# An eighth turned expert in position 1, and a first state tile prepared one step further at each place

## The chip, the cores and the metric

The kernel runs on one core of one Trainium2 chip. The metric is the time of one execution on the device, in microseconds; the median of three runs is 1242.97 us (1241.31 to 1243.07). The trace that is read here comes from one profiled execution of 1242.44 us.

## The reference, cut to what matters

The input is `x` of shape (4, 1024, 128) in float32. Three parts follow each other, each with a layer norm in front and a residual sum behind:

```python
x = x + 0.5 * ffn(layernorm(x))      # mixture of 8 experts
x = x + mamba(layernorm(x))          # a state-space layer with 16 states
x = x + 0.5 * ffn(layernorm(x))      # the same mixture again

# ffn
router = softmax(x @ w_router); gate = softmax(x @ w_gating / 0.1)
g = x @ w_gate[e]; u = x @ w_up[e]              # 128 -> 512, for each of 8 experts
expert_out[e] = (silu(g) * u) @ w_down[e]       # 512 -> 128
cw = router * gate / (sum(router * gate) + 1e-9)
out = sum over e of expert_out[e] * cw[e]

# mamba
xs, z = split(x @ W_in)                         # 256 channels each
xc = silu(causal_conv4(xs) + conv_b)
dt, B, C = split(xc @ W_x); dt = softplus(dt @ W_dt + b_dt)
h[t] = exp(dt * A) * h[t-1] + dt * xc * B       # 256 channels x 16 states, over 1024 steps
y = (sum over states of h * C + xc * D) * silu(z);  out = y @ W_out
```

## The kernel before, in words

**Tiles and positions.** The 4096 rows of `x` are eight tiles of 512 rows. Each tile goes through the mixture twice, which makes 16 positions; `ORDER` says which mixture (0 or 1) of which tile stands at each, and it starts with tiles 0 and 1 of the first mixture. A position has 8 experts of 4 slots each, so 32 slots; a slot is one chunk of 128 of the 512 inner columns. Experts are counted through: expert 8 is the first of position 1, with slots 32 to 35.

**A slot.** TensorE makes the gate product (`first_g`, L996 to L999) two slots ahead and the up product (`first`) of its own slot, each as three products of rounded float32 parts (high by high, low by high, high by low); ScalarE applies silu (`silu`, L1555); VectorE multiplies by the up product (`h`, L1345). The down product of a slot comes two slots later (`down`), in one of two forms. Not turned, it is 4 float32 products, 8 records of 128 columns in the trace at L1105. Turned, its result is transposed, and it is three products of 512 columns on rounded parts (L1097, L1099, L1101); for these the activations are split into a high part (`h_hi`, ScalarE L1566 or VectorE L1295) and a low part (`h_lo`, VectorE L1301), and each pair of slots splits its down weights (`wd_hi` L1572 or L1308, `wd_lo` L1313).

**Turned experts.** `TURNS` names them per position: before, experts 1 to 5 of position 0, 1 to 7 of position 1, all 8 of position 14 and 0 to 6 of position 15. The weighing of a turned expert (`acc`, L1279) multiplies by rows of router weights: after the position's weights are known they are transposed (`cw_t`, L1124), stored to DRAM (`cw_store`, L960) and loaded again, spread over all partitions, once per turned expert (`cw_load`, L967) into the ring `YE` of two buffers. The first turned expert of a position writes its product into `AT` itself; the others are added to `AT` by a transfer that GpSimd issues (L1721). At the end `AT` is transposed back and added to the rows (`t_tr` L1134, `t_add` L1290). An expert that isn't turned is weighed by L1338 or L1580 and added to `XT` by a transfer of the same size.

**The state-space layer.** For tile t the stream `before(t)` prepares it: layer norm, four products with `W_in` (`b_in`), the convolution (`b_conv`, L1396), silu, the product with `W_x` (L1148), the store and loads of B and C (L948, L955), the product with `W_dt` (L1155, L1156), softplus and `b_dx` (L1408). Then `scans(t)` takes over: for each state n a product (`s_b`, L1426), two scans (L1437), a product (`s_hc`, L1445), and the exponentials `s_da` on ScalarE (L1643, a table load and 4 instructions for two states).

**What sets the order.** The function `timetable()` writes one list of steps, and each engine's program is that list filtered to its own steps; every engine runs its part in order, with semaphores between. `timetable()` keeps an estimated clock for each engine, and the side streams (prep, before, scans, closing, rows, turn) are generators. `side()` is called after each gate, each up and each down of a slot. It advances the mixture's side streams; the stream `before` is otherwise advanced by `fill()`, and only while VectorE's estimated clock is less than about 1.4 us ahead of TensorE's. Steps that need a bank for small products share a single one (`NB` is 1), which `take()` hands out.

`WEIGHED_LATER` puts the weighing of a turned expert behind the next expert's second down, and of the first of a position (`BEGIN_LATER`) behind the third. SP's program holds the row loads and the loads of B and C in the order of the list, with waits for the store and for a free buffer.

Of the kernel before, what the change touches and what calls it, by code (L numbers as in the profile page):

```python
# [51 lines left out]
LATEST = 0.2  # L52
SIGNAL = {"pe": .14, "v": .12, "a": .15, "p": .1}
BURST = 2
HURRY = 0
QUICK = [("x2", NT - 1)]
FIRST_BY_VECTOR = (2, 3, 1)
SPARE = 1.0
# [14 lines left out]
NORMED = 5.0  # L73
PATIENCE = 25.0

TURNS = {0: range(1, 6), 1: range(1, 8), 14: range(0, 8), 15: range(0, 7)}
EASY = 0.8
SPLIT = 2
SPLITS = TURNS
TURNED = [p * E + e for p in TURNS for e in TURNS[p]]  # L80
SPLIT_EXPERTS = [p * E + e for p in SPLITS for e in SPLITS[p]]
TURN_BEGINS = {p * E + TURNS[p][0]: p for p in TURNS}
TURN_ENDS = {p * E + TURNS[p][-1]: p for p in TURNS}
SUMMING = (NPOS - 2, NPOS - 1)
TURN_SUMS = {p * E + TURNS[p][-1]: p for p in TURNS if p in SUMMING}
TURNED_SLOTS = {g * FC + c: k * FC + c for k, g in enumerate(SPLIT_EXPERTS) for c in range(FC)}
# [14 lines left out]
def timetable():  # L101
# [9 lines left out]
    def step(*what, after=0.0, **work):  # L111

        steps.append(what)
        for e, c in work.items():
            clock[e] = max(clock[e], after) + c
            after = clock[e] + SIGNAL[e]
        return after
# [62 lines left out]
    def prep(p):  # L180
# [29 lines left out]
        at = step("p_cw", p, after=at, v=.35)  # L210
        if p in TURNS:
            streams["rows"] = weights_rows(p, at)
# [32 lines left out]
    def weights_rows(p, at):  # L245
        yield from until(at + ROWS)
        bk = yield from take()
        at = step("cw_t", p, bk, after=at, pe=.15, a=.3)
        give(bk[0], "a_ct", list(TURNS).index(p) + 1, at)
        step("cw_store", p)  # L250
        rows_at[p] = at + 1.0
# [196 lines left out]
    def advance(k):  # L448
        if k not in streams:
            return None  # L450
        w = next(streams[k], "end")
        if w == "end":
            del streams[k]
        return w
# [17 lines left out]
    def side(but=None):  # L472
# [6 lines left out]
        turn[0] += 1  # L479
        if HURRY and "scans" not in streams and not begun["scans"]:  # L480
            advance("before")
# [1279 lines left out]
```

## Time and profile before

| what | value |
|---|---|
| median of 3 runs | 1242.97 us |
| the profiled execution | 1242.44 us |
| its span | 1240.6 us |
| TensorE busy | 1233.1 us (99%) |
| VectorE busy | 1143.4 us (92%) |
| ScalarE busy | 1003.6 us (81%) |
| GpSimd busy | 446.4 us (36%) |
| granted TensorE clock | 1.00 throughout |
| scans of tile 0 start | 161.49 us |

Times in the trace count from the start of the span. An engine's busy time is the union of its instructions; a matmul's end is modelled, so a short wait between two products can hide under a busy record and is better read from the starts of neighbouring products. The execution lies 0.5 us under the median of the three runs.

### The profile page before, as it was taken

Reading aid. Unit: us, or ns where it says so; the run is one execution under the profiler, and the core shown is the slowest. Engines: PE = TensorE matmul, PEld = TensorE weight load, DVE = VectorE, ACT = ScalarE, POOL = GpSimd, SP = SyncE. Lnnn points to the kernel's source line nnn. Section 1 sums busy time; section 2 is a strip of 40 time slices with the busy share of each in tenths; the row PEclk is TensorE's granted clock in tenths of the full one; section 3 lists DMA queues with packets and bytes.
Section 4 is the critical chain, followed back from the end, with each engine's and each line's share of the span. In section 5 each row is a group of like instructions: output and inputs, shape, how many; then the busy total and the mean of one; then the engine's idle time right before and its main releaser. Section 6 shows DMA issues by size and latency. Waiting matters only on the chain.

```text
span 1240.6 us, 20186 instructions
## 1 busy us (share of the span) xinstructions
PE 1233.1 (99%) x7072; PEld 1058.2 (85%) x7072; DVE 1143.4 (92%) x1368; ACT 1003.6 (81%) x2122; POOL 446.4 (36%) x571
## 2 busy tenths in 40 slices
PE   9999999999999999999999999999999999999999
PEld 7787788888888888888888888888888888887887
DVE  6958899999999999999999999997999999978877
ACT  7678789798898898988879898797988978846654
POOL 1021134445453463453434434452444344402000
PEclk9999999999999999999999999999999999999999
DMA  8412458888788997987889887986688979932322
GB/s 227 111 27 45 105 116 174 165 171 167 162 176 178 183 187 157 198 170 165 181 180 187 166 196 160 191 181 138 131 166 169 196 169 194 182 63 43 74 48 60
DMA packets 121015, 184.84 MB, mean 149 GB/s; under 512 B 11344, under 2 KB 38096, under 8 KB 120912
## 3 DMA queue, kind: packets, MB, share of 16 engines
q0 software_dynamic: 53568, 97.54, 45.0%
q1 hardware_dynamic: 67344, 86.00, 26.6%
q8 instruction: 56, 0.92, 0.3%
q14 instruction: 47, 0.39, 0.1%
HBM read 83.30 MB, written 2.69 MB: 69 GB/s over the span
## 4 chain that ended last, share of the span: by engine, by line
PE 93%; DVE 3%; ACT 2%; issue 1%; DMA 1%; SPq 0%; DVEq 0%; ACTq 0%
PE PS L1105 28%; PE PS L996 19%; PE PS L999 18%; PE PS L997 18%; PE PS L1101 2%; PE PS L1097 2%; PE PS L1099 2%; PE PS L1163 1%; PE PS L1148 1%; DVE HB L1345 1%; PE PS L1032 1%; DVE HL L1301 1%; PE PS L1040 1%; DMA YE<-CWD 1%; PE PS L1003 0%
## 5 line engine op out<-in xcount | busy, mean ns | idle before, releaser
L1105 PEld LDWEIGHTS PS<-WD,HB 128*128 128x128 f32 x3200 | 393.9, 191 | 22.1 <-issue 2.0
L1105 PE MATMUL PS<-WD,HB 128*128 128x128 f32 x3200 | 395.9, 275 | 0.0
L1345 DVE TENSOR_TENSOR HB<-PS,HB 128x1024 f32<-128x1024 f32 (+1 forms) x336 | 322.9, 962 | 72.5 <-PE PS L999 56.7
L1555 ACT ACTIVATE HB<-PS 128x512 f32<-128x512 f32 x512 | 294.9, 596 | 95.5 <-PE PS L999 93.5
L1733 POOL DMA_DIRECT2D Y<-HS x252 | 221.8, 954 | 317.6 <-DMA Y<-HS 151.7
L996 PE MATMUL PS<-XH,WG 128*128 128x512 f32 x509 | 219.7, 432 | 0.3 <-ACT HB L1555 0.2
L996 PE MATMUL PS<-XH,WU 128*128 128x512 f32 x512 | 204.4, 399 | 0.4 <-DVE HB L1345 0.4
L999 PE MATMUL PS<-XH,WU 128*128 128x512 f32 x512 | 201.2, 393 | 0.0
L999 PE MATMUL PS<-XH,WG 128*128 128x512 f32 x509 | 200.7, 394 | 0.1
L997 PE MATMUL PS<-XH,WU 128*128 128x512 f32 x512 | 200.4, 391 | 0.0
L997 PE MATMUL PS<-XH,WG 128*128 128x512 f32 x509 | 199.3, 392 | 0.0
L1721 POOL DMA_DIRECT2D XT<-YE x99 | 96.6, 976 | 197.7 <-ACT YE L1580 84.9
L1643 ACT ACTIVATE DA<-XS,aneg 128x512 f32<-128x512 f32 x256 | 164.1, 712 | 1.6 <-DVE HS L1437 1.0
L1437 DVE TENSOR_TENSOR_SCAN HS<-DA,car,HS 128x512 f32<-128x512 f32 x128 | 160.3, 1272 | 0.0
L1445 DVE TENSOR_TENSOR HS<-BCB,HS 128x1024 f32<-128x1024 f32 x128 | 156.3, 1221 | 2.4
L1426 DVE TENSOR_TENSOR HS<-BCB,DX 128x1026 f32<-128x1026 f32 (+1 forms) x128 | 155.8, 1221 | 1.6 <-DMA BCB<-BCD 1.5
L1437 DVE TENSOR_TENSOR_SCAN HS<-DA,HS 128x513 f32<-128x513 f32 x128 | 152.8, 1219 | 0.9 <-ACT DA L1643 0.8
L1566 ACT ACTIVATE HI<-HB 128x512 fp32r<-128x512 f32 x102 | 64.4, 632 | 76.1 <-DVE HB L1345 73.0
L996 PEld LDWEIGHTS PS<-XH,WU 128*128 128x128 f32 x512 | 96.1, 188 | 25.2 <-DVE HB L1345 3.1
L997 PEld LDWEIGHTS PS<-XH,WU 128*128 128x128 f32 x512 | 96.3, 188 | 21.7 <-issue 0.7
L999 PEld LDWEIGHTS PS<-XH,WU 128*128 128x128 f32 x512 | 96.1, 188 | 21.8
L999 PEld LDWEIGHTS PS<-XH,WG 128*128 128x128 f32 x509 | 95.5, 188 | 22.2 <-DVE XH L1403 0.5
(164 smaller groups left out, 1572.9 us busy)
## 6 DMA issues: line engine op xcount, KB each, us to landing
BCB<-BCD SPq DMA_DIRECT2D x128, 512.0 KB, 5.2
Y<-HS POOLq DMA_DIRECT2D x252, 256.0 KB, 6.0
XT<-YE POOLq DMA_DIRECT2D x99, 256.0 KB, 5.1
YE<-CWD SPq DMA_DIRECT2D x27, 256.0 KB, 4.5
AT<-YE POOLq DMA_DIRECT2D x21, 256.0 KB, 3.3
WD<-in_L_ffn_w_down_dram SPq DMA_DIRECT2D x8, 256.0 KB, 6.0
XT<-in_L_attn_x_dram SPq DMA_DIRECT2D x7, 256.0 KB, 5.8
out_dram<-XT SPq DMA_DIRECT2D x7, 256.0 KB, 5.4
```

Of the source, the lines that this page charges most:

```text
L996: pe.matmul(o, w[0], m[0], start=True, stop=False)
L997: pe.matmul(o, w[1], m[0], start=False, stop=False)
L999: pe.matmul(o, w[0], m[1], start=False, stop=True).then_inc(S[sem], 1)
L1105: z = pe.matmul(part(g, j), HB[:, i % NH, j * P:(j + 1) * P], WD[:, e, c, :], start=c == 0 and j == 0, stop=c == FC - 1 and j == SUB - 1)
L1345: v.tensor_tensor(H, PS[:, NG + i % 2:NG + i % 2 + n, :], H, ALU.mult).then_inc(S["v_h"], 1)
L1426: v.tensor_tensor(HS[:, m % HR, :, 0:w], rows.unsqueeze(1).broadcast_to([P, 2, w]), DX[:, t % 2, :, 0:w], ALU.mult).then_inc(S["v_db"], 1)
L1437: v.tensor_tensor_scan(H, DA[:, m % NA, j, 0:w], H, car[:, j, n:n + 1] if t % 2 else 0.0, ALU.mult, ALU.add).then_inc(S["v_sc"], 1)
L1445: v.tensor_tensor(H, BCB[:, m % BR, 1, :].unsqueeze(1).broadcast_to([P, 2, T]), H, ALU.mult).then_inc(S["v_hc"], 1)
L1555: a.activation(HB[:, i % NH, :], gate(i), ACT.Silu).then_inc(S["a_sil"], 1)
L1643: z = a.activation(DA[:, m % NA, j, 0:T], XS[:, t % 2, j, 3:3 + T], ACT.Exp, scale=aneg[:, j, n:n + 1])
L1721: gp.dma_start(to, buffer(g), accum_op=ALU.add).then_inc(S["c_acc"], 16)
L1733: gp.dma_start(Y[:, t % 2, j, :], HS[:, m % HR, j, 0:T], accum_op=ALU.add).then_inc(S[f"c_y{j}"], 16)
```

## The change

Two constants change. `TURNS[1]` becomes `range(0, 8)`, so expert 8 (slots 32 to 35) is turned as well: its down products take the other form, its activations and down weights are split, the first row load of position 1 is for expert 8, expert 8 writes `AT` at first, and expert 9 is added by a transfer to `AT`. Everything that is derived from `TURNS` follows. `HURRY` becomes 1, which makes a branch of `side()` live: as long as no scans stream exists and none has begun, each call of `side()` advances `before` by one step. The stream `before(1)` doesn't exist until scans have begun, so this is the preparation of state tile 0 alone.

```diff
-HURRY = 0
+HURRY = 1
...
-TURNS = {0: range(1, 6), 1: range(1, 8), 14: range(0, 8), 15: range(0, 7)}
+TURNS = {0: range(1, 6), 1: range(0, 8), 14: range(0, 8), 15: range(0, 7)}
```

The branch that it makes live stands in `side()`:

```python
        if HURRY and "scans" not in streams and not begun["scans"]:
            advance("before")
        elif "scans" in streams and (haste or turn[0] % (EVERY if passed[0] < SOONER else 1) == 0):
            advance("before")
        fill(clock["pe"] + LEAD + 1.0)
```

## Rows read from the trace of the kernel before

**Rows 1.** The page: span, busy time of the engines, the chain's shares, two groups.

```profile
span 1240.6 us, 20186 instructions
PE 1233.1 (99%) x7072; PEld 1058.2 (85%) x7072; DVE 1143.4 (92%) x1368; ACT 1003.6 (81%) x2122; POOL 446.4 (36%) x571
...
PE 93%; DVE 3%; ACT 2%; issue 1%; DMA 1%; SPq 0%; DVEq 0%; ACTq 0%
...
YE<-CWD SPq DMA_DIRECT2D x27, 256.0 KB, 4.5
```

**Rows 2.** Windows of the whole core: length, then busy us by engine, clock, DMA.

```profile
80.00:160.00 80.00, 78.96 (x368) 63.17 (x366) 65.02 (x124) 64.51 (x141) 13.72 (x27) 1.00 0.28 63
160.00:1080.00 920.00, 918.98 (x5594) 804.65 (x5594) 891.63 (x893) 795.90 (x1691) 403.19 (x493) 1.00 0.85 173
1080.00:1240.00 160.00, 157.08 (x752) 129.35 (x750) 128.14 (x228) 87.66 (x174) 20.03 (x29) 1.00 0.31 61
```

**Rows 3.** The chain in order of time: start, length, what; down products of two slots.

```profile
163.61 1.79 PE PS L1105 x16
```

**Rows 4.** Timeline where position 1 ends: start, length, instruction, [idle before <- releaser].

```profile
157.34 1.22 DVE L1426 TENSOR_TENSOR HS<-BCB,DX 128x1026 f32<-128x1026 f32 x1
157.85 0.39 PE L1097 MATMUL PS<-HI,WDS 128*128 128x512 f32 x1
158.47 1.22 DVE L1345 TENSOR_TENSOR HB<-PS,HB 128x1024 f32<-128x1024 f32 x1
158.53 0.39 PE L1097 MATMUL PS<-HI,WDS 128*128 128x512 f32 x1
158.75 2.56 ACT L1643 ACTIVATE DA<-XS,aneg 128x512 f32<-128x512 f32 x4
158.75 0.39 PE L1099 MATMUL PS<-HI,WDS 128*128 128x512 f32 x1
159.61 0.68 DVE L1301 TENSOR_TENSOR HL<-HB,HI 128x512 fp32r<-128x512 f32 x1
160.34 0.50 PE L1101 MATMUL PS<-HL,WDS 128*128 128x512 f32 x1 [1.20 <-DVE HL L1301]
```

**Rows 5.** Groups of VectorE by form, 90 to 155 us: busy, mean ns, idle before.

```profile
L1345 DVE TENSOR_TENSOR HB<-PS,HB 128x512 f32<-128x512 f32 x27 | 18.6, 687 | 11.8 <-PE PS L999 11.8
L1301 DVE TENSOR_TENSOR HL<-HB,HI 128x512 fp32r<-128x512 f32 x26 | 17.7, 682 | 0.0
L1313 DVE TENSOR_TENSOR WDS<-WD,WDS 128x256 fp32r<-128x256 f32 x14 | 6.0, 429 | 0.3
```

**Rows 6.** Position 0: its first row load and who waits for it, timeline of 30 to 44 us.

```profile
38.53 0.69 DVE L1279 TENSOR_TENSOR AT<-PS,YE 128x512 f32<-128x512 f32 x1 [1.11 <-DMA YE<-CWD]
39.75 0.39 PE L1099 MATMUL PS<-HI,WDS 128*128 128x512 f32 x1
40.48 0.50 PE L1101 MATMUL PS<-HL,WDS 128*128 128x512 f32 x1 [0.34 <-DVE HL L1301]
```

**Rows 7.** Position 1: store and first load of rows, VectorE from 100 us on, first use.

```profile
95.07 0.32 SPq L960 DMA_DIRECT2D CWD<-LR  x1
96.53 0.36 SPq L967 DMA_DIRECT2D YE<-CWD  x1
...
100.33 0.68 DVE L1301 TENSOR_TENSOR HL<-HB,HI 128x512 fp32r<-128x512 f32 x1
111.49 0.68 DVE L1279 TENSOR_TENSOR AT<-PS,YE 128x512 f32<-128x512 f32 x1
```

**Rows 8.** The preparation of state tile 0, and ScalarE's first burst of exponentials.

```profile
109.62 0.74 DVE L1396 SCALAR_TENSOR_TENSOR Y<-XS,cw_t,Y 128x512 f32<-128x512 f32 x1
113.95 0.74 DVE L1396 SCALAR_TENSOR_TENSOR Y<-XS,cw_t,Y 128x512 f32<-128x512 f32 x1
150.20 1.22 DVE L1408 TENSOR_TENSOR DX<-XS,Y 128x1024 f32<-128x1024 f32 x1
157.45 1.28 ACT L1643 ACT_TABLE_LOAD   x1
```

## The prediction

> **What bounds the kernel now.** I read the page first: TensorE is busy 1233.1 of 1240.6 us and has 93% of the chain that ended last, so 7.5 us of the span at most are waits that show as idle time [rows 1]. The windows say where they lie: 1.04 us in 80 to 160 us, only 1.02 us in the 920 us after it, 2.9 us in the last 160 [rows 2]. VectorE is the second full engine, at 97% from 160 to 1080 us, but only 81% in 80 to 160 us [rows 2]: this is position 1's stretch, where the change sits, and nearly all of VectorE's idle time there ends when a TensorE product is done (11.8 us, before `h`) [rows 5]. So VectorE waits for TensorE here, and the time follows TensorE: its work, plus every wait that gets through to it. Waits are read from neighbouring starts: where a third down product follows its second by more than 0.23 us, the rest is lost.
>
> **Part 1, expert 8 turned: what goes.** Two slots of the unturned down take 1.79 us [rows 3], so 0.895 us a slot. A turned slot takes from 157.85 to 158.53, 0.68 us for its three products [rows 4]. Four slots: 4 x 0.215 = 0.86 us less on TensorE, which is the path. Nothing is late in their place by itself, since the gate and up products of the next slots are already at hand in order.
>
> **Part 1, what comes on VectorE and ScalarE.** Four low parts of the activations, 4 x 0.68, and two low parts of down weights, 2 x 0.43, are 3.6 us on VectorE [rows 5]; the high parts go to whichever engine the timetable finds free. They fall between 80 and 93 us. VectorE has 15 us idle in 80 to 160 us [rows 2], a share of 19%, so some 2.5 us in those 13 us and 3.6 wanted: it becomes full there, for 1 us of lag at most, and a `h` or a low part has about 1 us of room before the third product wants it. I cost it at 0.1 us; bounds are 0 and, if that cover is gone, one wait like the largest in position 1, 159.61 to 160.34 behind a late low part, 1.36 us by starts (1.59 - 0.23) [rows 4]. Transfers are a wash: expert 8's transfer to XT goes and expert 9's to AT comes, one issue each on GpSimd; SP gets one row load more.
>
> **Part 1, a wait that is added.** This is the term that I looked at longest. Before, the first row load of position 1 was issued at 96.53, landed about 4.5 us later, and was used only at 111.49 [rows 7, 1]: ten microseconds of room. Now it serves expert 8, weighed behind the third down of expert 9, that is behind the low part that ran at 100.33 and ended about 100.93 [rows 7]. With TensorE 0.86 us ahead, VectorE arrives at 100.1. The store is triggered by a step with a due time 4 us behind the router weights, so it moves little: the load lands at 101.0. VectorE waits 0.9 us. Queued behind it in order are the weighing, state tile 0's low part (`b_xl`), a weight split and the `h` and low part of the next slot, for which TensorE's down waits. Position 0 has the same figure: VectorE waited 1.11 us for its first row load, and TensorE then lost 40.48 - 39.75 - 0.23 = 0.50 us [rows 6]. Bounds: 0 (the store moves forward by the same 0.86 us, and no wait is left) and 1.0 (a second wait of that size in the wake). I take 0.35 us, scaled from position 0 by 0.9/1.11 and rounded down for the earlier store.
>
> The store of the rows is followed by its load after 96.53 - 95.07 = 1.46 us, since SP waits for the landing [rows 7]. The Trainium skill, in "DMA: Bandwidth & Descriptors", section "Anatomy of one DMA — SWDGE (gpsimd) path", gives any DMA a fixed cost of about 2.0 us, heaviest where the target is HBM, as here. By that rule the pair would land 0.5 us later, the wait of VectorE would be 1.4 us and the term 0.6 instead of 0.35; this trace's store is quicker than the page has it, and it is the same store, so the row decides.
>
> **Part 2, `HURRY`.** It removes and adds no instruction. It moves the steps of `before(0)` ahead of others in the queues of VectorE, ScalarE and TensorE, and on SP the store and first loads of B and C ahead of a row load or two. How far: the first two taps of the convolution, which need nothing of each other, stand 4.3 us apart (109.62, 113.95) [rows 8], because `fill()` stops when VectorE's clock is ahead. With a step at each call they come some 0.7 us apart, and the third product with `W_in` gets the bank before the next position's preparation does. From 113.95 to the end of the preparation at 150.20 [rows 8] are 36 us for work of which VectorE's share is small. I estimate the preparation done 8 to 12 us earlier. But scans can run then only in VectorE's idle time, and that is 15 us in the window less 3.6 for part 1, so all of the state-space work gains at most 11 us, and I count with 5. What is that worth? From 160 to 1080 us TensorE loses 1.0 us in all [rows 2]: an earlier state-space layer has nothing to give to an engine that doesn't wait for it. It can only give back waits near the place itself. The largest of them is at the end of position 1: VectorE began `s_b` of the second state at 157.34, the doubled `h` behind it started at 158.47 and the low part at 159.61, and TensorE's third product came 1.36 us late [rows 4]. Without that `s_b` in front, `h` could start about 1.0 us earlier. If the hurried order puts it elsewhere 1.0 us is gained; but a doubled `h` with a low part behind it stands at this border anyway, and some scan work will stand near it. On the other side the scans of tile 0 now start inside turned slots, of which rival C tells. Bounds: -1.4 (that wait gone) and +4.1 (rival C). I take 0, between them and nearest to the windows, where the larger part of the scans' 920 us costs TensorE nothing.
>
> The one other cover that I lean on is the shared SP queue: row loads wait for a free buffer and loads of B and C stand behind them. Before, the first use of a row load came 10 us after its landing [rows 7], so a load or two of B and C ahead of one is hidden; gone, it would be a wait like position 0's, 0.50 us [rows 6].
>
> **Part 3, everything behind.** The timetable is greedy, so all later choices (which engine weighs, where a burst of exponentials stands) may fall otherwise. The work stays. The waits there are 1.0 + 2.9 us [rows 2]; I expect their sum back within 0.6 us either way.
>
> **The sum**, against the profiled execution, 1242.44 us, span 1240.6: -0.86 + 0.1 + 0.35 + 0 = -0.41, so 1242.0 and a span of 1240.2. That execution is 0.53 us below the median of the three runs; on the median it is 1242.97 - 0.41 = 1242.6. I predict 1242.5.
>
> **Rivals.**
> A. The row load is in time, and the border's wait goes: -0.86 + 0.1 - 1.2 = -2.0, 1241.0. For it: VectorE has 15 us idle in the window. Against: position 0's first load was late in the same construction [rows 6]. Chance 0.21.
> B. The row load costs its upper bound and the splits theirs: -0.86 + 1.0 + 1.36 = +1.5, 1244.5. For it: a full queue on VectorE with `b_xl` just behind. Against: VectorE was idle half a microsecond or more before most `h` in this stretch [rows 5]. Chance 0.13.
> C. Slower. The scans of tile 0 begin inside position 1, and with them ScalarE's bursts of exponentials: a table load of 1.28, 2.56 for four and, to return to silu, a second load of the same kind, 5.1 us in which no silu and no high part is made [rows 8, 4]. A turned slot needs ScalarE for both, and TensorE's products for two slots are shorter by 2 x 0.215 us. The single burst so far that touches turned slots is the one at 157.45, and the largest wait in position 1 stands beside it [rows 4]. Decays for two states at a time are allowed up to three states ahead of the scans, so up to three bursts can come before slot 64: 3 x 1.36 = 4.1. With the sum's other terms 1242.97 - 0.41 + 4.1 = 1246.7. It decides from about 2.9 us of added waits on, two bursts at full price and a bit. Against: the timetable hands high parts to VectorE when ScalarE is behind, and the wait at 160.34 is named after VectorE. Chance 0.13.
> D. `HURRY` doesn't do what it says: `before` was advanced at nearly every place already, or the one bank holds it, and scans start where they did. Then the sum is part 1's alone, 1242.6 as well. Chance 0.10. My forecast has the other 0.43.
>
> **How the numbers follow.** A measurement of this kernel can tell about 0.2% from no change, 2.5 us: below 1240.5 is faster, above 1245.5 slower. The forecast, D and B lie between. Of A's 0.21 I put 0.10 below 1240.5, where also waits behind 160 us get fewer. Of C 0.12 lies above 1245.5, of B 0.02. Faster 0.10, same 0.76, slower 0.14. The range goes from 1240.4 (the removed work, the border's wait and 0.4 of part 3) to 1245.6 (B's bounds and part of C), which leaves 0.1 out at either end.
>
> **What would show it.** Right: 16 L1105 records fewer per two slots, 32 in all, and 4 more each of L1097, L1099, L1101, L1301; L1279 of expert 8 at 100 to 101 us with idle time that ends on YE<-CWD; a gap of about 0.5 us between a second and third down product before 105 us; DX (L1408) at 138 to 143 instead of 150.20; all of the state-space work up to 5 us earlier and the window 160 to 1080 us as full as before. Wrong: gaps of over 1 us at third down products between 135 and 160 beside L1643 (C); the gap at the border gone with the first load in time (A); DX where it was (D); or TensorE's idle time behind 160 us grown by more than 0.6 us, which no part of this sum has.

## The result, and the profile after

| | before | after |
|---|---|---|
| median, 4 runs each | 1242.55 us | 1258.26 us |
| lowest and highest | 1241.31, 1243.07 | 1252.23, 1258.55 |
| profiled span | 1240.6 us | 1256.5 us |
| mean granted clock of TensorE | 1.00 | 0.996 |

The ratio is 1.0116, with a 95% interval of 1.0085 to 1.0148. By the medians it is slower by 15.7 us, where 1242.5 was forecast and 1245.6 was the upper end of the range. One of the four runs took 1252.23 us, at a clock of 0.997.

The page of the kernel after, its lines that answer to [rows 1] (busy time of each engine; the chain of waits by engine):

```profile
span 1256.5 us, 20163 instructions
...
PE 1237.4 (98%) x7052; PEld 1059.0 (84%) x7052; DVE 1150.4 (92%) x1383; ACT 1001.6 (80%) x2116; POOL 453.3 (36%) x571
...
PE 69%; DMA 11%; DVE 7%; ACT 6%; issue 4%; POOL 2%; SPq 0%; DVEq 0%; POOLq 0%; ACTq 0%
```

TensorE's busy time grew by 4.3 us although 0.86 us of work is gone, and the rest of the 15.9 us is idle time. The chain that ended last now runs through transfers for 11% of the span, 1% before. The windows answer to [rows 2], cut finer (length; busy us of PE, PEld, VectorE, ScalarE, GpSimd; clock; DMA share; GB/s):

```profile
80.00:120.00 40.00, 36.40 (x161) 28.81 (x160) 27.71 (x57) 26.98 (x65) 4.76 (x11) 0.96 0.13 32
120.00:160.00 40.00, 39.84 (x170) 30.82 (x170) 35.33 (x70) 31.53 (x71) 7.63 (x15) 1.00 0.31 64
160.00:200.00 40.00, 33.57 (x181) 28.68 (x180) 30.87 (x33) 28.82 (x59) 11.77 (x13) 0.91 0.55 116
200.00:1096.00 896.00, 892.81 (x5432) 780.52 (x5432) 872.14 (x874) 772.14 (x1636) 402.96 (x487) 1.00 0.85 174
```

Two windows of 40 us hold most of it, and only these two have a clock under 1.00. VectorE's waits from 80 to 200 us, longest in total first, name what is late (who waits, for whom: us in total, times, longest):

```profile
DVE HB L1345 <- PE PS L999: 12.2, 15, 1.6
DVE YE L1279 <- DMA YE<-CWD: 5.4, 1, 5.4
DVE AT L1279 <- DMA YE<-CWD: 4.1, 1, 4.1
DVE aneg L1370 <- ACT aneg L1584: 1.4, 1, 1.4
```

The first line is VectorE waiting for TensorE, in 15 short waits. Both long waits are loads of router rows: the first of position 1 (expert 8's), which the forecast had at 0.9 us, and one for expert 14, which it had at nothing.

**The first wait.** SP's, VectorE's and TensorE's timelines of the kernel after, around expert 8's weighing:

```profile
97.83 0.32 SPq L960 DMA_DIRECT2D CWD<-LR  x1
...
104.15 0.40 PE L999 MATMUL PS<-XH,WU 128*128 128x512 f32 x1
105.89 0.69 DVE L1279 TENSOR_TENSOR AT<-PS,YE 128x512 f32<-128x512 f32 x1 [4.10 <-DMA YE<-CWD]
106.63 0.50 PE L1097 MATMUL PS<-HI,WDS 128*128 128x512 f32 x1 [2.08 <-DVE AT L1279]
106.97 0.40 PE L1099 MATMUL PS<-HI,WDS 128*128 128x512 f32 x1
107.83 0.64 PE L1101 MATMUL PS<-HL,WDS 128*128 128x512 f32 x1 [0.46 <-DVE HL L1301]
108.27 0.63 PE L996 MATMUL PS<-XH,WG 128*128 128x512 f32 x1
108.70 0.63 PE L997 MATMUL PS<-XH,WG 128*128 128x512 f32 x1
```

and the chain of waits there (start, length, what):

```profile
97.83 3.49 DMA CWD<-LR
101.32 0.01 issue
101.33 4.53 DMA YE<-CWD
```

The store started 2.8 us later than before and took 3.49 us against 1.46 [rows 7]; the load behind it took its usual 4.5. By starts TensorE loses 106.63 - 104.15 - 0.23 = 2.25 us, since the down product wants the bank that the weighing empties, and 107.83 - 106.97 - 0.23 = 0.63 behind the next low part. Then eight products start 0.43 us apart instead of 0.23 (108.27, 108.70): the granted clock has gone from its level of 2.4 GHz to that of 1.2 GHz, for 1.6 us more. A third wait stands ahead of them: VectorE waited 1.37 us at 90.42 behind a table load on ScalarE, and TensorE lost 1.2 us at 90.72.

**The second wait.** SP's, VectorE's and TensorE's timelines of the kernel after, where position 1 ends:

```profile
151.03 0.32 SPq L948 DMA_DIRECT2D BCD<-XN  x1
152.66 1.39 SPq L955 DMA_DIRECT2D BCB<-BCD  x3
154.09 13.68 SPq L967 DMA_DIRECT2D YE<-CWD  x2
...
164.37 0.39 PE L1099 MATMUL PS<-HI,WDS 128*128 128x512 f32 x1
167.57 0.69 DVE L1279 TENSOR_TENSOR YE<-PS,YE 128x512 f32<-128x512 f32 x1 [5.36 <-DMA YE<-CWD]
168.18 1.22 DVE L1408 TENSOR_TENSOR DX<-XS,Y 128x1024 f32<-128x1024 f32 x1
169.31 1.22 DVE L1345 TENSOR_TENSOR HB<-PS,HB 128x1024 f32<-128x1024 f32 x1
170.45 0.68 DVE L1301 TENSOR_TENSOR HL<-HB,HI 128x512 fp32r<-128x512 f32 x1
171.19 0.79 PE L1101 MATMUL PS<-HL,WDS 128*128 128x512 f32 x1 [6.43 <-DVE HL L1301]
171.78 0.63 PE L996 MATMUL PS<-XH,WG 128*128 128x512 f32 x1
172.21 0.63 PE L997 MATMUL PS<-XH,WG 128*128 128x512 f32 x1
```

The row load of 256 KB was issued right behind three loads of B and C of 512 KB each, and landed 13.46 us later, at 167.55. VectorE waited 5.36 us with `b_dx`, a doubled `h` and a low part queued behind, so TensorE lost 171.19 - 164.37 - 0.23 = 6.59 us, and then some 2.1 at the lower clock. The product that waited is the last one of slot 63, behind the doubled `h` and its low part: the place where the kernel before lost 1.36 us [rows 4]. So 5.2 us of the 6.59 are new.

Why not before? The same stretch of the kernel before, SP and VectorE:

```profile
139.03 0.32 SPq L948 DMA_DIRECT2D BCD<-XN  x1
140.88 1.38 SPq L955 DMA_DIRECT2D BCB<-BCD  x3
142.31 1.33 SPq L967 DMA_DIRECT2D YE<-CWD  x1
...
156.74 0.68 DVE L1279 TENSOR_TENSOR YE<-PS,YE 128x512 f32<-128x512 f32 x1
```

The load was slow there too: it landed at 151.96, 9.65 us after its issue, and was used at 156.74, so it had 4.8 us of room. In the kernel after VectorE was ready for this weighing at 162.21 (167.57 - 5.36), 5.5 us later than before. But the load was issued 11.8 us later (154.09 for 142.31) and took 3.8 us longer, so it came 10.1 us later against the weighing; 4.8 of these were room, the rest is the wait.

It was issued late because SP runs its list in order. The buffer of this load was free at 146.60, when the transfer of expert 12 landed that GpSimd had issued at 143.31. But the store of B and C stands ahead of the load, and that one went out at 151.03 instead of 139.03. So the load was held for 7.5 us, where it was held for 1.8 in the kernel before (the transfer issued at 137.26 landed at 140.54).

**The account.** TensorE's lost time, from the starts of neighbouring products minus the median spacing of their kind, in us by window:

| kernel | 0–80 | 80–120 | 120–160 | 160–200 | behind 200 | sum |
|---|---|---|---|---|---|---|
| before | 1.9 | 0.2 | 1.9 | 0.5 | 2.7 | 7.2 |
| after | 2.2 | 6.2 | 0.7 | 9.0 | 5.6 | 23.7 |

The difference is 16.4 us; with 0.86 us of removed work that leaves 15.6, and the spans differ by 15.9. The windows are of time and not of work: slot 63's wait lies in 120 to 160 us before and in 160 to 200 us after.

### The profile page after: what moved, and what is told of

Read it like the earlier page. It is cut to its first block, busy times and chain, and to the rows that moved or that the text cites. A ratio compares the mean times of both kernels' runs of the same rounds, so it can differ in the third digit from the quotient of the medians.

```text
span 1256.5 us, 20163 instructions
## 1 busy us (share of the span) xinstructions
PE 1237.4 (98%) x7052; PEld 1059.0 (84%) x7052; DVE 1150.4 (92%) x1383; ACT 1001.6 (80%) x2116; POOL 453.3 (36%) x571
## 4 chain that ended last, share of the span: by engine, by line
PE 69%; DMA 11%; DVE 7%; ACT 6%; issue 4%; POOL 2%; SPq 0%; DVEq 0%; POOLq 0%; ACTq 0%
PE PS L1105 19%; PE PS L996 14%; PE PS L999 14%; PE PS L997 14%; DMA Y<-HS 7%; DVE HB L1345 2%; DMA YE<-CWD 2%; PE PS L1101 2%; PE PS L1097 1%; PE PS L1099 1%; DMA XT<-YE 1%; DVE HS L1437 1%; ACT DA L1643 1%; ACT HB L1555 1%; PE PS L1148 1%
## 5 line engine op out<-in xcount | busy, mean ns | idle before, releaser
L1105 PEld LDWEIGHTS PS<-WD,HB 128*128 128x128 f32 x3168 | 389.3, 191 | 20.9 <-issue 1.5
L1105 PE MATMUL PS<-WD,HB 128*128 128x128 f32 x3168 | 391.0, 275 | 0.0
```

Source lines behind the costliest of these rows:

```text
L1105: z = pe.matmul(part(g, j), HB[:, i % NH, j * P:(j + 1) * P], WD[:, e, c, :], start=c == 0 and j == 0, stop=c == FC - 1 and j == SUB - 1)
```

## The experiments

The explanation to test: the time went into two waits of VectorE for row loads, each of which also costs clock; the one in 80 to 120 us comes from expert 8 and its late store, the one behind 160 from the three loads of B and C ahead of the row load. Rivals: the bursts of exponentials inside turned slots (rival C of the prediction), VectorE too full by expert 8's splits, and the replanned order as such. The ratios stand against runs of the kernel before on the same chip.

| kernel | median us | ratio, 95% | 80–120 | 120–160 | 160–200 | behind 200 |
|---|---|---|---|---|---|---|
| expert 8 alone | 1253.46 | 1.0091 [1.0076, 1.0106] | 6.2 | −0.2 | 5.0 | 5.7 |
| `HURRY` alone | 1258.54 | 1.0129 [1.0114, 1.0144] | 0.4 | 8.3 | 6.5 | 5.6 |
| after, two B/C loads later | 1252.23 | 1.0092 [1.0066, 1.0118] | 4.1 | 0.6 | 2.7 | 6.5 |
| after, expert 8's rows ahead | 1252.53 | 1.0082 [1.0067, 1.0097] | 1.5 | 6.6 | 1.8 | 5.5 |
| both of these | 1247.96 | 1.0039 [1.0025, 1.0053] | 1.4 | 1.7 | 4.1 | 3.1 |
| `HURRY` alone, B/C loads later | 1252.1 | 1.0073 [1.0058, 1.0088] | 0.4 | 2.1 | 5.4 | 5.2 |
| before, replanned only | 1245.58 | 1.0019 [1.0010, 1.0028] | 0.2 | 1.8 | 0.4 | 3.4 |
| expert 8, order kept | 1243.07 | 0.9999 [0.9991, 1.0008] | 0.7 | 2.0 | 0.4 | 3.4 |
| the same, border moved | 1241.81 | 0.9990 [0.9981, 0.9999] | 0.6 | 1.0 | 0.4 | 3.3 |
| border moved alone | 1241.94 | 0.9994 [0.9985, 1.0002] | 0.2 | 0.8 | 0.5 | 2.7 |

The last four columns are the lost time of the profiled execution in us, as above. Four runs of one kernel lie up to 7.7 us apart here ("after, two B/C loads later": 1250.26 to 1257.92), and the medians of different chips stand side by side, so single microseconds between two rows say little.

**Each half alone.** The kernel after with `-HURRY = 1` / `+HURRY = 0`:

> Expert 8 turned, HURRY back to 0. Theory 1 (late row loads): the loss comes from row loads that land after VectorE has reached the weighing that needs them, once at expert 8 (4.10 us of wait in the kernel after) and once at expert 14, whose load stands in SP's queue behind the first three loads of B and C (5.36 us). Without HURRY the preparation of tile 0 ends later still, so the three loads of B and C come a few us later and stand before the load of expert 15 instead: a wait of the same kind there. 1250 to 1260 us. Rival (the hurried order does the damage, by filling VectorE's and ScalarE's queues in turned slots): the sum of my prediction without it, 1242 to 1244 us. DX (L1408) at 165 us or later in both.

and the kernel after with position 1's experts as before:

```diff
-TURNS = {0: range(1, 6), 1: range(0, 8), 14: range(0, 8), 15: range(0, 7)}
+TURNS = {0: range(1, 6), 1: range(1, 8), 14: range(0, 8), 15: range(0, 7)}
```

> HURRY 1, expert 8 not turned. Theory 1: no row load is used early here; the first one of position 1 serves expert 9, ten microseconds after landing, and the loads of B and C are issued about 10 us earlier, when the row load behind them has some 8 us of room. 1241.5 to 1244 us, no wait over 0.5 us of VectorE on YE<-CWD, DX (L1408) at 138 to 143 us. Rival (the hurried order): most of the loss is here, 1250 us or more, at third down products between 135 and 160 us.

Neither half is harmless: 1.0091 and 1.0129. For `HURRY` alone 1241.5 to 1244 us had been expected, and that was missed. Expert 8 alone has both waits, the second at expert 15. VectorE's timeline of that kernel:

```profile
105.49 0.69 DVE L1279 TENSOR_TENSOR AT<-PS,YE 128x512 f32<-128x512 f32 x1 [4.26 <-DMA YE<-CWD]
169.25 0.69 DVE L1279 TENSOR_TENSOR YE<-PS,YE 128x512 f32<-128x512 f32 x1 [5.66 <-DMA YE<-CWD]
169.85 1.22 DVE L1408 TENSOR_TENSOR DX<-XS,Y 128x1024 f32<-128x1024 f32 x1
```

So `b_dx`, the end of tile 0's preparation, goes from 150.20 [rows 8] to 169.85 by expert 8 alone, and `HURRY` takes back 1.7 us of it (168.18). But in both kernels `b_dx` stands on VectorE behind the second wait, and some 5.5 us of the delay are that wait itself. The store of B and C, issued ahead of that wait, tells how late the preparation is: 139.03 before, 154.41 with expert 8 alone, 151.03 after. SP's, VectorE's and TensorE's timelines of `HURRY` alone:

```profile
129.69 0.32 SPq L948 DMA_DIRECT2D BCD<-XN  x1
131.32 1.39 SPq L955 DMA_DIRECT2D BCB<-BCD  x3
132.75 1.36 SPq L967 DMA_DIRECT2D YE<-CWD  x1
144.37 0.69 DVE L1279 TENSOR_TENSOR YE<-PS,YE 128x512 f32<-128x512 f32 x1 [4.25 <-DMA YE<-CWD]
145.64 1.22 DVE L1408 TENSOR_TENSOR DX<-XS,Y 128x1024 f32<-128x1024 f32 x1
167.63 1.23 DVE L1437 TENSOR_TENSOR_SCAN HS<-DA,HS 128x513 f32<-128x513 f32 x1 [2.77 <-ACT DA L1643]
170.62 0.80 PE L1101 MATMUL PS<-HL,WDS 128*128 128x512 f32 x1 [3.41 <-DVE HL L1301]
```

Alone it does what it says, and about as far as the prediction had it: the store of B and C goes out 9.3 us earlier (129.69 for 139.03). `b_dx` itself gains only 4.6 (145.64 for 150.20), since the wait of 4.25 us stands in front of it. And being early breaks the fit too: the B and C loads move to 131.32, ahead of a row load that is wanted at 140, and it lands at 144.34. Its buffer was free at 124.16, so it was held for 8.6 us. Behind it a scan beside turned slots waits 2.77 us for its exponentials, with a doubled `h` and its low part queued behind. That is rival C's mechanism, once, for 3.57 us of TensorE at 166.83, again at slot 63, where 1.36 had been lost before.

**The B and C loads.** The kernel after with one load of B and C ahead of the row load instead of three:

```diff
-            bc_loads(BR)
+            bc_loads(1)
```

> The kernel after, but of the first three loads of B and C only one is issued ahead of the row loads of experts 14 and 15, the other two behind them. Nothing else in any engine's order changes. Theory 1: the wait at expert 14 (5.36 us of VectorE, 6.59 us by starts on TensorE, and the half clock behind it, some 2.2 us) goes: 1258.3 - 8.8 = 1249.5; perhaps 1 us of it returns, because the second product of the scans now waits for its load. 1248.5 to 1252 us. Rival (ScalarE's burst of exponentials beside that wait is the cause): unchanged, 1257 to 1259.

SP's and TensorE's timelines of this kernel:

```profile
104.11 0.40 PE L999 MATMUL PS<-XH,WU 128*128 128x512 f32 x1
106.11 0.50 PE L1097 MATMUL PS<-HI,WDS 128*128 128x512 f32 x1 [1.61 <-DVE AT L1279]
...
150.54 0.36 SPq L955 DMA_DIRECT2D BCB<-BCD  x1
150.94 6.79 SPq L967 DMA_DIRECT2D YE<-CWD  x2
157.78 3.14 SPq L955 DMA_DIRECT2D BCB<-BCD  x2
```

The second wait is gone (of VectorE's waits for row loads from 80 to 200 us only the first is left, 3.6 us), with 6.3 us of lost time in 160 to 200 us, and slot 63 loses 1.12 us, where the kernel before loses 1.36. The median falls by 6.0 us; the slowest of the four runs still took 1257.92. The row load landed 5.21 us after its issue, at 156.15, and was used at 160.01. This edit moves only those two loads, so without them ahead of the row load there is no wait. It doesn't follow that they alone make it: the row load was held behind the late store here too, for 6.4 us. Issued at 146.60 in the kernel after, even a landing time of 13.46 us would have brought it at 160.1, before the 162.21 at which VectorE wanted it (an estimate from the two kernels' rows). So by this estimate both were needed, the late store and the loads behind it. A row load ahead of the store was not tried. The first wait, 1.77 us by starts here, cost no clock in this execution, the quickest of the kernel's four. The same edit on the kernel with `HURRY` alone:

> HURRY alone, with two of the first three loads of B and C behind the next row loads. HURRY alone took 1258.5: a wait of 4.25 us of VectorE at L1279 for a row load issued at 132.75 behind those three (5.6 us by starts on TensorE), 3.6 us at the end of position 1 where a scan waits for exponentials, the half clock after both, and 3 us behind 300 us. Theory 1: the first goes, with its half clock some 7 us: 1251.5; the other stays. 1249 to 1253 us. Rival (the hurried steps fill VectorE's queue, the row load only happened to be late there): 1256 to 1259.

It takes 6.2 us from 120 to 160 us and 6.4 us from the time, and here all four runs (1250.82 to 1252.8) lie below all four without the edit (1258.1 to 1259.85). The wait of the scan for its exponentials stays, with 3.57 us of TensorE, now at 161.27.

**The first row load.** In the kernel after, expert 8 is weighed with position 0's rows, which are long in DRAM, loaded ahead of the store:

```diff
                 elif s[0] == "cw_store":
+                    if s[1] == 1:
+                        wt.wait_ge(S["c_ct"], 16)
+                        wait_buffer(wt, E)
+                        rows = CWD[0].rearrange("(j e) p -> e j p", e=E)[1:2]
+                        sy.dma_start(buffer(E), rows.broadcast_to([P, SUB, P])).then_inc(S[rows_loads(E)[0]], 16)
...
+                elif s[0] == "cw_load" and s[1] == E:
+                    pass
```

> The kernel after, but expert 8's rows are loaded from the rows that position 0 stored, so ahead of position 1's store and not behind its landing; expert 8 is weighed with position 0's weights, a part of the output that this kernel leaves wrong. No other instruction moves. Theory 1: the wait of 4.10 us at L1279 goes, and with it 2.25 + 0.63 us by starts on TensorE and the half clock behind (8 products at 0.2 us more, 1.6 us): 1258.3 - 4.5 = 1253.8. The later wait at expert 14 stays. Rival (VectorE is simply full between 100 and 107 us): 1257 to 1259.

80 to 120 us falls from 6.2 to 1.5 us of lost time: the first wait was the row load's, and the clock fell behind it. The second wait stays, and only changes its window: its row load, again behind three loads of B and C, goes from 149.30 to 162.28, and TensorE loses 6.12 us from 159.56 on, where after lost 6.59 from 164.37 on. The median falls by 5.7 us (runs 1251.25 to 1255.41). With both edits:

> The kernel after with both edits at once: expert 8's rows taken from position 0's store, ahead of position 1's (expert 8 is weighed with position 0's weights, which this kernel leaves wrong), and two of the first three loads of B and C behind the row loads of experts 14 and 15. Theory 1 (late row loads plus the half clock behind them are the loss): alone they gave 6.0 and 5.7 us back; what is left over the kernel before is 1.2 us at 90 us, where VectorE waits for ScalarE's table loads, 1.1 us at the end of position 1, and some 4 us of new waits behind 400 us, less 0.86: 1247.5 to 1250 us, granted clock 1.00. Rival (the waits are replaced by others, since VectorE and ScalarE are full there): 1252 or more, as each edit alone.

1247.96 us, 10.3 us less than after, with every run below every run of after: 4.5 us are left over the runs of before on the same chip, of 15.7. The two waits with their clock are some two thirds of the loss. What is left is a wait of 1.2 us at 89.79, one of 2.47 at 167.58 (the closing transposition waits for a transfer to `AT`), and small ones; the 1.14 at 158.80 are slot 63's, which the kernel before has too. The wait of 2.47 may come from the edit: the transfer of expert 14 was issued at 157.55, beside the two loads of B and C that were moved, and took 8.8 us instead of 3.3, and the last transfer was issued only behind it, at 166.91.

**The replanned order.** The kernel before with one constant that only shifts where the planner calls `before` once scans run:

```diff
-EVERY = 3
+EVERY = 4
```

> The kernel before with one constant of the timetable moved, EVERY 3 to 4: no expert more is turned and no step is hurried; the order is the same up to 190 us and falls otherwise behind. It measures what a replanned order costs by itself. Theory 2 (the kernel before has an order that was picked for having hardly a wait, and nearly any other has more): 1244 to 1248 us, with 2 to 5 us of new waits before L1032, L1345 or L996 spread over positions 3 to 13. Rival (the order is robust, the late waits of the kernel after come from its late state-space layer): 1242 to 1243.5.

The ratio is 1.0019 [1.0010, 1.0028] over 10 runs, some 2.4 us, for a new order alone; its profiled execution shows 0.9 of them as lost time. The kernel after has waits of that kind, at places that the change doesn't touch. At 445.33, for one, TensorE waits 1.06 us for a normed tile (L1032, behind ScalarE's L1525).

The kernel after and five of the experiments on it or on one half lose 5.2 to 6.5 us behind 200 us, where before loses 2.7; the one with both waits off (3.1) and the control (3.4) lose less. The kernel with both waits off has the same order behind 200 us as the kernel after, since its edits move only row loads and loads of B and C ahead of that. So the 2.9 us that after loses there more than before aren't a fixed price of its order; how much of them is the order's, and how much follows from what came before, is open. The control shows that a new order alone can cost time, 1.2 to 3.5 us by its interval.

**Expert 8 with the order kept.** The planner's list of the kernel before, into which expert 8's steps are put by hand (behind the named step, the new ones):

```diff
+    behind = {("down", 29): [("wd_hi", 32), ("wd_lo", 32)],
+              ("h", 32, 1): [("h_hi", 32)],
+              ("h", 33, 1): [("h_hi", 33), ("h_lo", 32, 1)],
+              ("h", 34, 1): [("h_lo", 33, 1), ("h_hi", 34)],
+              ("down", 32): [("wd_hi", 34), ("wd_lo", 34)],
+              ("h", 35, 1): [("h_lo", 34, 1), ("h_hi", 35)],
+              ("h", 36, 1): [("h_lo", 35, 1)],
+              ("h_lo", 40, 1): [("acc", 8)]}
```

> Expert 8 turned inside the order of the kernel before: its steps are inserted by hand into the old timetable (row load first behind the store, weighing behind the low part of slot 40), and no other step moves. Theory: the 0.86 us of TensorE work come back in full, since the row load lands at 101 us and VectorE reaches the weighing at 102 to 103, and the 3.6 us of VectorE work fit its idle time; no replanned order, so no new wait behind. 1241.5 to 1242.0 against 1242.6. Rival (turning expert 8 costs waits wherever it is put, as position 1 has no room on VectorE): 1243 to 1246.

The ratio is 0.9999 [0.9991, 1.0008], over 11 runs; the 0.6 to 1.1 us less that were expected don't show. But the work of expert 8's turn isn't what costs, and neither is a full VectorE. SP's and VectorE's timelines of this kernel:

```profile
98.19 0.91 SPq L967 DMA_DIRECT2D YE<-CWD  x2
...
104.20 0.68 DVE L1279 TENSOR_TENSOR AT<-PS,YE 128x512 f32<-128x512 f32 x1
```

The load starts 3.1 us earlier than in the kernel after and the weighing finds it there. The 0.86 us of saved work are lost again in small waits (0.5 us more in 80 to 120, 0.7 behind 200, 0.4 ahead of 80).

**The border.** The forecast's largest wait of position 1 [rows 4], at slot 63, with `s_b` of the second state moved behind the last low part; on the kernel above, and alone:

```diff
+    steps.remove(("s_b", 0, 1))
+    steps.insert(steps.index(("h_lo", 63, 1)) + 1, ("s_b", 0, 1))
```

> Expert 8 turned inside the order of the kernel before, as in the run of that name, and one step more moved by hand: the product of the scans (L1426) that stood in front of the doubled `h` at the end of position 1 goes behind that `h` and the low part after it. The wait there (1.33 us by starts) shrinks by the 1.1 us that the product takes, and 0.86 us of TensorE work is gone: 1.0 us less than the run without the move and 1.0 to 1.9 us less than the kernel before (the run without the move showed the 0.86 us hardly or not: 0.9999 [0.9991, 1.0008]). Rival (what is gained at the border is lost a few slots on, because the first scan begins later): the same as the kernel before.

> The kernel before with that one step moved, nothing else. 1.0 us less than the kernel before, gap at the border about 0.3 us instead of 1.36, if that wait is worth what the gap says; the first scan starts at its old time, as it waits for the weighing of expert 15 and ScalarE's exponentials. Rival: no change.

TensorE's and VectorE's timelines of the border moved alone:

```profile
158.61 1.22 DVE L1345 TENSOR_TENSOR HB<-PS,HB 128x1024 f32<-128x1024 f32 x1
159.95 0.39 PE L1099 MATMUL PS<-HI,WDS 128*128 128x512 f32 x1
160.35 1.22 DVE L1426 TENSOR_TENSOR HS<-BCB,DX 128x1026 f32<-128x1026 f32 x1
160.49 0.50 PE L1101 MATMUL PS<-HL,WDS 128*128 128x512 f32 x1
```

The third product follows 0.54 us behind the second instead of 1.59: 1.05 us are gone there, and the time is 1.0 us below the 21 runs of before on that chip (1242.98), at an interval that still reaches 1.0002. With expert 8 it is 1.2 us, 0.9990 [0.9981, 0.9999]. That is the best version found, and 0.1% under the kernel before.

## Why the prediction was wrong

Three statements failed, two in Part 2 and one in Part 1.

1. *"I estimate the preparation done 8 to 12 us earlier."* It came later: the store of B and C by 12.0 us (151.03 for 139.03), of which some 5.5 are the lateness of the whole kernel by then, and `b_dx` by 18.0 (168.18, foreseen at 138 to 143), of which 5.4 are the second wait. For `HURRY` by itself the estimate was good (9.3 us at the store). What was missed is expert 8, which the prediction priced on the engines and not in the planner's clocks: with it alone the store is 15.4 us later. Already the first layer norm of the preparation (L1511) came at 99.75 instead of 89.24, and `b_xl` (L1376) at 121.31 instead of 100.93. How the delay passes through the planner is read from its code; no kernel tried it. `timetable()` holds back steps that need ScalarE while ScalarE's estimated clock is over 1 us ahead of TensorE's, and a high part enters that clock only once VectorE's clock has reached its `h`. So VectorE's clock, filled by the low parts, carries over. The lists fit this: `timetable()` puts `b_dx` at 150.7 on VectorE's clock in the kernel before and at 156.8 in the kernel after, at 149.0 if expert 8's low parts are given no time, and still at 156.8 if its high parts are given none.

2. *"Before, the first use of a row load came 10 us after its landing [rows 7], so a load or two of B and C ahead of one is hidden; gone, it would be a wait like position 0's, 0.50 us [rows 6]."* That room was read at the first load of position 1 and used for one that stands behind three B and C loads, which had 4.8 us. And the price was that of a load behind nothing. With 1.5 MB ahead of it the load took 9.65 us before and 13.46 after, and it was held behind the late store for 7.5 us instead of 1.8. TensorE lost 6.59 us, 5.2 more than before at this slot, plus 2.1 of clock, against a price of 0.50. Moving two of the three loads gave 6.0 us of the median back.

3. *"The store is triggered by a step with a due time 4 us behind the router weights, so it moves little: the load lands at 101.0."* It landed at 105.86. This is the first wait, and the term of +0.35 below.

By the other steps:

- **Removed work, −0.86:** right in its count (L1105 has 3168 records, 32 fewer). In time it is hardly there: expert 8 with the order kept lies 0.35 us below the runs of before on its chip (1243.42), and with the border moved expert 8 adds 0.13 us of gain, both inside the intervals.
- **Splits, +0.1:** the mechanism (VectorE lags) shows in none of the long waits, and the kernel with the order kept has only 0.5 us more lost in the window. Right to within that.
- **The first row load, +0.35 (bound 1.0):** the mechanism was right in place, instruction and releaser, and the size was wrong by more than ten: 2.25 + 0.63 us of waits and 1.6 of clock. The load did land 4.5 us after its issue. The step that failed is "it moves little": the store was issued 2.8 us later (97.83 for 95.07) and took 2.0 us more. The order kept gives the price without that: no wait at all. The Trainium skill's page "DMA: Bandwidth & Descriptors", section "Anatomy of one DMA — SWDGE (gpsimd) path", with its fixed cost of about 2.0 us, would have moved this term by 0.25 us only. The section describes transfers that GpSimd issues, and this store is one of SP's, which the prediction passed over. The store of the kernel after, at 3.49 us, lies above both that figure and the 1.46 us of before.
- **A term that was missing, the clock:** half speed behind both long waits, some 3.7 us together. The kernel before is at 1.00 throughout, so its rows could not price it.
- **Everything behind, ±0.6:** +2.9 us. The bound came from a kernel whose order had been left as it was; the replanned control costs 2.2 us by the medians, though its trace shows only 0.7 of it as lost time behind 200 us.
- **The border's wait:** rival A was right that it can go, for 1.05 us, when it is moved by hand. In the kernel after it didn't go: the second wait fell on the same product, the third of slot 63, and took it in. Rival C's mechanism exists, once, in `HURRY` alone. Rival D is refuted in the form in which it stood: `HURRY` does move the preparation.
- **TensorE's idle time behind 160 us grown by more than 0.6 us:** named as a sign of a wrong sum, and it came.

The accounting by parts: the first wait and its neighbours +6.0 us, 120 to 200 us with the second wait +7.3 (+8.5 and −1.2, as slot 63 changed its window), behind 200 us +2.9, before 80 us +0.3, work −0.86.

Open: why one run of the kernel after took 1252.23 us; the four runs of the kernel with two B and C loads later also lie between 1250.26 and 1257.92, at mean clocks of 1.000 and 0.996. So the clock may have fallen in some runs and not in others, but only one run of each kernel has a trace. Open as well is why the row load took 13.46 us after its issue and 9.65 before, behind the same three loads.

## What to carry to other kernels

In a statically planned kernel an edit of one stage is priced by what the planner's clocks do with it, not only by its instructions: put the edit into the old order by hand and compare, and run a replanned control. The room of a load is to be read at that load, with what stands ahead of it on its queue: both what holds back its issue and what slows its landing. A long wait on TensorE cost a further 1.6 to 2.1 us in clock here, so waits don't simply add up. And a wait that seems to leave one window of time may only have moved to the next: compare the same slot.

## What was not expected of the hardware

- **A small store that landed late.** Position 1's store of the rows landed after 1.38 to 1.51 us in the kernel before and in the six experiments that keep its order there or only hurry, expert 8 put in by hand among them, and after 2.86 to 3.49 us in the kernel after and the four experiments with expert 8 planned in. In the kernel after, one packet of 16 KB on the queue of instruction fetches started at 98.86 and took 1.43 us, and the store's last packets of data started only at 100.27 and 100.33. Such a packet stands within each of the five slow stores, and within none of the seven fast ones. That the fetch is the cause was not tried.
- **The clock.** After TensorE had lost 2.25 us (104.15 to 106.63) and 6.6 us, products of 512 columns came 0.43 us apart instead of 0.23, for 8 and 11 products. After 1.77 us (104.11 to 106.11, two B and C loads later) the same stretch stayed at 1.00.
- **Loads of B and C.** Behind three loads of 512 KB, issued within 1.4 us, a 256 KB load landed after 9.2 to 13.5 us (nine kernels); behind one of them after 5.2 to 5.8 (three kernels), and the median of all is 4.7. Beside them a transfer by GpSimd, issued at 155.37 in the kernel after, took 12.0 us, where the median of its kind is 3.3.
